# Recurrence: operands of 32 and 64 rows padded to 128 rows with zeros, and the receptance product issued ahead of the output products

## The reference, cut to what matters

```python
shifted = pad(h, one step);  delta = shifted - h
x_lerp = h + delta * x_proj_mu
x0 = tanh(x_lerp @ xl_w1.T) @ xl_w2.T + xl_b2        # 256 -> 32 -> 160
x1 = tanh(x0).reshape(B_, T_, 5, 32)
x2 = einsum('btnr,hnr->btnh', x1, x_out_w.reshape(H_, 5, 32))
r_mu, w_mu, k_mu, v_mu, g_mu = x2 + x_bias
r = (h + delta * r_mu) @ r_w.T                        # receptance, 256 -> 128
w = tanh((h + delta * w_mu) @ w_w1.T) @ w_w2.T + w_b  # 256 -> 64 -> 128
k, v, g = ... in the same way, 256 -> 128, 256, 256
wd = exp(-exp(w))                                     # per head of 32 keys
for each token:                                       # 4 heads, DK 32, DV 64
    o_t = r_t . S + sum(r_t * bonus * k_t) * v_t
    S = S * w_t + k_t v_t
out = (norm(o) * gn_weight + gn_bias) * silu(g) @ o_w.T
```

## Time and profile before

| | us |
|---|---|
| median of 3 runs | 5183.19 (5174.28 to 5184.97) |
| the profiled execution | 5169.71 |
| its span, first to last instruction | 5168.1 |
| PE busy in the span | 4565.2 (88%) |
| DVE busy | 2719.6 (53%) |
| ACT busy | 1988.2 (38%) |
| POOL busy | 1665.3 (32%) |
| mean granted clock of TensorE | 0.909 |

### The profile page before, as it was taken

One profiled execution on the slowest core, in us unless ns is written; L12 is line 12 of the kernel. 1 busy time (PEld: TensorE's weight loads), 2 busy tenths in 40 slices (PEclk: granted clock), 3 DMA queues, 4 the chain that ended last, 5 costly groups with the idle time before them and its releaser, 6 DMA issues. The chain is left out here.

```text
span 5168.1 us, 80399 instructions
## 1 busy us (share of the span) xinstructions
PE 4565.2 (88%) x29148; PEld 3603.7 (70%) x29148; DVE 2719.6 (53%) x5127; ACT 1988.2 (38%) x3685; POOL 1665.3 (32%) x1322
## 2 busy tenths in 40 slices
PE   6605999999999999799999999999997798888885
PEld 6604988988989899466666666666665677777774
DVE  4484333333333343365555555555554477777775
ACT  2203454444444444143333333333333343434431
POOL 1103444434344443332322222322332223333333
PEclk9999999999999999788887888888887899999998
DMA  6622322223232222100000000000000434433432
GB/s 207 219 94 66 50 53 57 44 57 59 39 63 41 60 42 36 32 21 17 22 17 22 17 18 21 22 17 17 21 17 16 132 83 99 97 91 89 99 66 37
DMA packets 246853, 294.07 MB, mean 57 GB/s; under 512 B 19041, under 2 KB 223585, under 8 KB 242401
## 3 DMA queue, kind: packets, MB, share of 16 engines
q0 software_dynamic: 85760, 117.74, 13.3%
q1 hardware_dynamic: 135136, 137.74, 8.3%
q10 hardware_dynamic: 25600, 33.56, 1.9%
HBM read 154.62 MB, written 134.35 MB: 56 GB/s over the span
## 5 line engine op out<-in xcount | busy, mean ns | idle before, releaser
L578 DVE TENSOR_TENSOR e_hTl<-e_hf,e_hTh 128x512 fp32r<-128x512 f32 x512 | 355.0, 694 | 775.0 <-ACT e_hTh L521 774.9
L1031 POOL TENSOR_TENSOR a_mix<-a_tmp,a_h 128x512 f32<-128x512 f32 x320 | 384.1, 1217 | 993.0 <-DVE a_tmp L1090 845.7
L442 POOL DMA_INDIRECT acc_d<-e_y,e_sids x256 | 402.4, 1572 | 723.8 <-DVE e_y L594 678.9
L520 ACT ACTIVATE e_hf<-ps_heads,e_b 128x512 f32<-128x512 f32 x512 | 353.2, 690 | 645.0 <-PE ps_heads L665 641.7
L665 PE MATMUL ps<-e_w2h,e_hTh 128*128 128x256 f32 x2048 | 585.7, 286 | 0.0
L665 PE MATMUL ps<-e_w2h,e_hTl 128*128 128x256 f32 x2048 | 583.6, 285 | 0.0
L665 PE MATMUL ps<-e_w2l,e_hTh 128*128 128x256 f32 x2048 | 577.7, 282 | 0.0
L665 PE MATMUL ps_heads<-e_xTh,e_w1h 128*128 128x512 f32 x1024 | 419.6, 410 | 41.6 <-ACT e_hTh L521 28.9
L665 PE MATMUL ps_heads<-e_xTh,e_w1l 128*128 128x512 f32 x1024 | 408.7, 399 | 0.0
L665 PE MATMUL ps_heads<-e_xTl,e_w1h 128*128 128x512 f32 x1024 | 407.7, 398 | 0.0
L665 PEld LDWEIGHTS ps<-e_w2h,e_hTh 128*128 128x128 f32 x2048 | 392.9, 192 | 19.8
(11 more groups left out here) (287 smaller groups left out, 10089.4 us busy)
## 6 DMA issues: line engine op xcount, KB each, us to landing
r_x<-in_L_attn_hidden_states SPq DMA_DIRECT2D x32, 512.0 KB, 3.8
xn_d<-r_xn ACTq DMA_DIRECT2D x32, 512.0 KB, 3.1
xnT_d<-r_xT ACTq DMA_DIRECT2D x32, 512.0 KB, 3.4
acc_d<-r_zeros POOLq DMA_DIRECT2D x16, 1024.0 KB, 21.1
e_w<-in_L_ffn_w SPq DMA_DIRECT2D x16, 1024.0 KB, 4.9
s_d<-a_s SPq DMA_DIRECT2D x32, 512.0 KB, 2.9
f_a<-acc_d SPq DMA_DIRECT2D x32, 512.0 KB, 3.8
f_x<-s_d SPq DMA_DIRECT2D x32, 512.0 KB, 5.2
```

Of the source, the lines that this page charges most:

```text
L442: pool.indirect_dma_start(acc_d, bass.IndirectOffsetOnAxis(ap=sids[:, GT * q + t:GT * q + t + 1], axis=0), ys[r][:, t, :], None, compute_o ...
L520: nc.scalar.activation(hf[m % 2][:], ps[2 + m % 2][:], ACT.Gelu, bias=b1s[:, m:m + 1])
L578: nc.vector.tensor_tensor(hT[q % 2][1][:, m, :], hf[m % 2][:], hT[q % 2][0][:, m, :].bitcast(F32), ALU.subtract).then_inc(h_sb, 1)
L1031: nc.gpsimd.tensor_tensor(mix[n][:, m, :].rearrange("p (c t) -> p c t", c=GT), tmp[i % 2][:].rearrange("p (c t) -> p c t", c=GT), h[q % 2] ...
```

## The change

The weights `w2`, `xot`, `dw2` and the activations `low`, `x1t`, `dlow` become tiles of 128 rows. GpSimd zeroes all of each first, the loads and ScalarE then write only the first 32 or 64 rows, and TensorE reads all 128. Three loads move behind that zeroing, beside the loads of `xo`. Piece 5 keeps only `REC` (with `rk` and the copy to R) and runs ahead of chunk step 0 in slot 7. Its two mixes become piece 6, behind chunk step 0 in the same slot, and the later pieces are numbered one higher.

```diff
-        w2 = sb("a_w2", [RANK, NMU * RANK])
+        w2 = sb("a_w2", [P, NMU * RANK])
-        xot = sb("a_xot", [RANK, D])
+        xot = sb("a_xot", [P, D])
-        dw2 = sb("a_dw2", [GATE, KW])
+        dw2 = sb("a_dw2", [P, KW])
-        low = sb("a_low", [RANK, GN])
+        low = sb("a_low", [P, GN])
-        x1t = sb("a_x1t", [RANK, GN])
+        x1t = sb("a_x1t", [P, GN])
-        dlow = sb("a_dlow", [GATE, GN])
+        dlow = sb("a_dlow", [P, GN])
...
+        PADDED = 7
+        SET = PADDED + 8
+        READY = SET + NH + 2
...
-        FRONT = SLOTS - LATE
+        FRONT = SLOTS - LATE + 1
...
-        AT = {2: (0, 1), 3: (2, 3), 4: (4, 5), 5: (6, 7), 6: (8, 9)}
+        AT = {2: (0, 1), 3: (2, 3), 4: (4, 5), 6: (6, 7), 7: (8, 9)}
...
                     elif left:
-                        piece(g + 1, f1[1], s - LATE, False)
+                        piece(g + 1, f1[1], s - LATE if s < CHUNK else s - LATE + 1, False)
 
                 for s in range(SLOTS):
                     if s < LEVELS:
                         level(g, r, s, first)
+                    if left and s == CHUNK:
+                        piece(g + 1, f1[1], CHUNK - LATE, False)
...
-            sp.wait_ge(set_up, 9)
-            for n in range(NMU - 1):
-                sp.dma_start(xo[RANK * n:RANK * (n + 1), n, :], w["L0_attn_x_out_w"][RANK * n:RANK * (n + 1)]
-                             ).then_inc(w_in, 16)
+            padded = [(w2[0:RANK, :], w["L0_attn_xl_w2"]), (dw2[0:GATE, :], w["L0_attn_w_w2"]),
+                      (xot[0:RANK, :], w["L0_attn_x_out_w"][P:P + RANK])]
+            padded += [(xo[RANK * n:RANK * (n + 1), n, :], w["L0_attn_x_out_w"][RANK * n:RANK * (n + 1)])
+                       for n in range(NMU - 1)]
+            sp.wait_ge(set_up, PADDED)
+            for dst, src in padded:
+                sp.dma_start(dst, src).then_inc(w_in, 16)
...
-            nc.gpsimd.memset(xo[:], 0.0).then_inc(set_up, 1)
+            for operand in (xo, w2, xot, dw2, low, x1t, dlow):
+                nc.gpsimd.memset(operand[:], 0.0).then_inc(set_up, 1)
...
-                    nc.scalar.activation(low[:], ready(LOW)[0:RANK, :], ACT.Tanh).then_inc(act_out, 1)
+                    nc.scalar.activation(low[0:RANK, :], ready(LOW)[0:RANK, :], ACT.Tanh).then_inc(act_out, 1)
...
-                if s == 6:
+                if s == 7:
...
-                if s == 7:
+                if s == 8:
...
-                if s == 8:
+                if s == 9:
```

More of the change, by code:

```diff
@@ L932, in _ @@
         def _(sp):
-            loads = [(mu[:], w["L0_attn_x_proj_mu"]), (w1[:], w["L0_attn_xl_w1"]), (w2[:], w["L0_attn_xl_w2"]),
+            loads = [(mu[:], w["L0_attn_x_proj_mu"]), (w1[:], w["L0_attn_xl_w1"]),
                      (b2[:], w["L0_attn_xl_b2"][0:P]), (b2t[:], w["L0_attn_xl_b2"][P:P + RANK]),
-                     (xot[:], w["L0_attn_x_out_w"][P:P + RANK]), (xb[:], w["L0_attn_x_bias"]),
+                     (xb[:], w["L0_attn_x_bias"]),
                      (rw[:], w["L0_attn_r_w"]), (kw[:], w["L0_attn_k_w"]), (vw[:], w["L0_attn_v_w"]),
-                     (gw[:], w["L0_attn_g_w"]), (dw1[:], w["L0_attn_w_w1"]), (dw2[:], w["L0_attn_w_w2"]),
+                     (gw[:], w["L0_attn_g_w"]), (dw1[:], w["L0_attn_w_w1"]),
                      (db[:], w["L0_attn_w_b"]), (bonus[:], w["L0_attn_bonus"]),
@@ L941, in _ @@
                 sp.dma_start(dst, src).then_inc(w_in, 16)
-            sp.wait_ge(set_up, 9)
-            for n in range(NMU - 1):
-                sp.dma_start(xo[RANK * n:RANK * (n + 1), n, :], w["L0_attn_x_out_w"][RANK * n:RANK * (n + 1)]
-                             ).then_inc(w_in, 16)
-            assert len(loads) + NMU - 1 == LOADS + 1
+            padded = [(w2[0:RANK, :], w["L0_attn_xl_w2"]), (dw2[0:GATE, :], w["L0_attn_w_w2"]),
[5 more added lines that the diff above has]
+                sp.dma_start(dst, src).then_inc(w_in, 16)
+            assert len(loads) + len(padded) == LOADS + 1
             def load(j, q, first):
@@ L1000, in _ @@
             nc.gpsimd.iota(row[:], pattern=[[0, P]], base=0, channel_multiplier=1).then_inc(masks, 1)
-            pool.wait_ge(set_up, 9)
+            pool.wait_ge(set_up, SET)
             pool.wait_ge(masks, 2)
@@ L1004, in _ @@
                 nc.gpsimd.memset(heads[hd * DK:(hd + 1) * DK, hd:hd + 1], 1.0).then_inc(set_up, 1)
-            pool.wait_ge(set_up, 13)
+            pool.wait_ge(set_up, SET + NH)
             pool.wait_ge(w_in, 16 * (LOADS + 1))
@@ L1008, in _ @@
             nc.gpsimd.tensor_scalar(gnb[:], gnb[:], 0.5, None, ALU.mult).then_inc(set_up, 1)
-            pool.wait_ge(set_up, 15)
+            pool.wait_ge(set_up, READY)
             def ahead(f, j, q):
@@ L1062, in _ @@
                                               ALU.add))
-            dve.wait_ge(set_up, 15)
+            dve.wait_ge(set_up, READY)
             def ahead(f, j, q):
@@ L1163, in _ @@
             act.wait_ge(w_in, 16 * (LOADS + 1))
-            act.wait_ge(set_up, 15)
+            act.wait_ge(set_up, READY)
             def ahead(f, j, q):
@@ L1179, in piece @@
                 if s == 0:
-                    nc.scalar.activation(low[:], ready(LOW)[0:RANK, :], ACT.Tanh).then_inc(act_out, 1)
+                    nc.scalar.activation(low[0:RANK, :], ready(LOW)[0:RANK, :], ACT.Tanh).then_inc(act_out, 1)
                 if s == 1:
                     nc.scalar.activation(x1[:], ready(X0)[:], ACT.Tanh, bias=b2[:, 0:1]).then_inc(act_out, 1)
-                    nc.scalar.activation(x1t[:], ready(X0T)[0:RANK, :], ACT.Tanh, bias=b2t[:, 0:1]).then_inc(act_out, 1)
+                    nc.scalar.activation(x1t[0:RANK, :], ready(X0T)[0:RANK, :], ACT.Tanh, bias=b2t[:, 0:1]).then_inc(act_out, 1)
                 if s == 3:
-                    nc.scalar.activation(dlow[:], ready(DLOW)[0:GATE, :], ACT.Tanh).then_inc(act_out, 1)
+                    nc.scalar.activation(dlow[0:GATE, :], ready(DLOW)[0:GATE, :], ACT.Tanh).then_inc(act_out, 1)
                 if s == 4:
@@ L1277, in _ @@
             pe.wait_ge(w_in, 16 * (LOADS + 1))
-            pe.wait_ge(set_up, 15)
+            pe.wait_ge(set_up, READY)
             pe.wait_ge(vw_centred, 3)
```

## The result

The changed kernel took 4873.62 us (median of 4 runs, 4872.36 to 4875.07). The kernel before took 5178.73 on the same chip (4 runs, 5167.5 to 5184.97). The ratio is 0.9415, 95% interval 0.9404 to 0.9427, so the change is faster by 5.9%. The forecast was 4884 us (range 4855 to 4985), and 4871 for an execution like the profiled one. The profiled execution's span is 4870.7 us with a mean granted clock of 0.965 (before: 5168.1 and 0.909).

What follows compares the result with a forecast made beforehand. Bound: TensorE, busy but at clock 0.82 in the recurrence. Savings 270.8 + 8 + 6.3 (clock) + 14.9 + 1 (wait) - 1.9 (set-up) = 299 us, giving 4871 for the profiled execution, 4884 as median; range 4855 to 4985.

Steps and rivals of the forecast that it cites:

- The step: Recurrence: full-row padding keeps TensorE's clock at 1.00 in all 28 turns, saving 270.8 us.
- both falls: Half-clock stretches per turn, about 6.7 us behind `low` products and 13.4 behind `OWN` and `x1t` products; both forecast to go.
- the one good turn of before: Group-loop turn from 2216.52 in the earlier trace: 48.34 us at clock 1.00, model for all turns after the change.
- zero rows are not counted: Rival at the padded products: clock ignores zero rows, only the wait goes; 5169, up to 5185 us; 8 in 100.
- The padding: Five products per group with zero rows added: no change in their own cost, range -8 to +13 us over 31 groups.
- The order: Receptance product ahead of chunk step 0: 0.68 us wait for R's copy goes, 14.9 us saved over 28 turns.
- The new wait before `OWN`: After mixes 6 and 7, TensorE waits for VectorE to empty the bank: 0.15 us per turn.
- Set-up: GpSimd zeroes 2080 more columns ahead of the index patterns, delaying the first product: 1.9 us lost.
- One fall stays: Rival in the turns: 4974 us if the first half-clock stretch stays, 5064 if the second; 9 in 100.
- `REC` never waited for its operands: Rival after the keys: TensorE waits for GpSimd's late adds, 5222 us with the clock unchanged; 3 in 100.
- The first rival: Padded products' zero rows do not count for the clock, only the wait goes: 5169, up to 5185 us; 8 in 100.
- a length that holds itself: Recurrence turns of 58.03 us, mean 58.01 over 28, might keep that length despite the removed wait: up to 5185 us.

Runs made afterwards that it cites:

- The unrolled kernel: Loop over token blocks 1 to 6 written out, against the changed kernel: 4854.25 us, ratio 0.9382 to the kernel before.
- the unrolled kernel of before: Loop over token blocks 1 to 6 written out, nothing else changed, against the kernel before: 5159.75 us, ratio 0.9962.
- the measured kernel: The change's new order of products alone, nothing padded, against the kernel before: 5075.49 us, ratio 0.9816.

## Why the prediction was right

*The clock.* The step held, and by its size: both falls went in every one of the 28 turns. The one short fall at 3309.4 stands at the loop boundary and is of another kind. All turns at 1.00 were forecast to be like the one good turn of before, less the wait: 47.8 us. They came to 47.78 in the mean. That products with 96 zero rows in the moving operand as well keep the clock is now shown by the padded kernels. The rival "zero rows are not counted" is out.

*That mean hides three errors that cancel, and that they cancel is luck.* A turn outside the loop is 47.20, 1.14 below the good turn of the earlier trace rows, where 0.53 was forecast. The padding was booked at nothing and gives 48.34 - 47.97 = 0.37: half of it at the 64-row product, half at `low`, nothing at `x1t`. My bound of 0.24 to the good side was too narrow because I compared the products' own durations, not the starts of their neighbours. The order gives 0.77, not 0.53. The new wait before `OWN` that I had put at 0.15 did not come, and about 0.1 more came off the interval of `OWN`. Against that stands a cost that was not in the sum: the loop. 28 turns at 47.20 would be 1321.6 us, and the 28 took 1337.8. The unrolled kernel shows these 16 us to be the loop's: some 1.3 to 1.6 at each boundary, 0.3 a turn inside it, and the fall at 3309.4 with 1.7. In the trace of before no wait at the boundary exists, and my good turn lay ahead of the loop, so neither showed it. At half clock the second stretch lay over the boundary and covered the stall. The kernel with only `low` padded shows this: no stall at the four boundaries under such a stretch, 1.4 us at the one without. That the unrolled kernel of before gained something all the same comes mostly with its three turns that lost falls or parts of them.

*Set-up.* The first product is at 2129.62 against 2127.70: 1.9 us, as forecast. By `OWN` of the first group 0.9 of it is left.

*The rest of the sum.* Between `OWN` of group 0 and of group 3, 8.0 us were gained (9 forecast), and from `OWN` of the last group to the end of the span 3.7 (6.3 forecast, for the window of the earlier trace rows alone; the later levels gave some back). Together 286.6 + 8.0 + 3.7 - 0.9 = 297.4.

*The rivals.* "One fall stays" did not happen, but when made to happen it cost 6.25 and 3.31 a turn against 6.4 and 3.2. `REC` never waited for its operands. The first rival's time was wrong in itself, though: with both falls left and only the wait taken out I had 5169 to 5185, and the measured kernel took 5075. The words "a length that holds itself" were nearer than I used them. 58.03 us was a repeating pattern, and a turn shortened by 0.65 us leaves it, in either of two unrelated ways. Had the zero rows not counted, I would have been 95 us off.

## What to carry to other kernels

Compare turns of a loop at equal clock before blaming waits. Where TensorE is busy and yet at 1.2 GHz, look which products stand ahead of each fall, and try full rows of zeros there: it costs a few memsets. Take the price of a fall from one stretch at either level, and expect the clock's recovery to lay bare small waits and loop boundaries that it had covered. A timing gain on a kernel with periodic falls can be the pattern shifting rather than the work removed: check it with a second, unrelated shortening.

## What was not expected of the hardware

- Removing 0.65 us of wait per turn saved 67 and 103 us over 31 turns (5174 to 5107 and 5178 to 5075), by letting whole turns run at 1.00 with the same 32-row products inside.
- A 64-row product between ones of 128 rows cost 0.10 us in its own interval and 0.10 in its successor's. The 32-row products of `low` cost 0.10 in their predecessor's and 0.09 in their own, and those of `x1t` nothing (1.91 us either way).
- Turns inside a register loop run 0.3 us longer than the same turns written out (47.50 and 47.20), and a boundary at the full clock stalls TensorE by 1.4 to 1.8 us once per iteration (7.8 us in five). Under a stretch at half clock it cost nothing.
